# Fewer unread TensorE products in two loops of a graph kernel

## The reference

```
# relational attention, for each of five edge types r
e      = leaky(Qn[tgt] @ a_q + Kn[src] @ a_k)
e_exp  = exp(e - segment_max(e, tgt)[tgt])
attn   = e_exp / (segment_sum(e_exp, tgt)[tgt] + 1e-10)
h     += segment_sum(mask * Vn[src] * attn, tgt)
...
# typed attention, eight heads of 16 features
ex     = exp(scores - segment_max(scores, dst)[dst])
den    = segment_sum(ex, dst)
agg    = segment_sum(V[src] * ex / (den[dst] + 1e-10), dst)
```

## Time and profile before

| what | value |
|---|---|
| median of 3 runs | 4971.89 us (4968.58 to 4981.04) |
| the profiled execution's own time | 4978.06 us |
| its span, first to last instruction | 4976.0 us |
| mean granted TensorE clock over the span | 0.734 |
| TensorE busy / weight loads | 3122.3 us (63%) / 2741.5 us (55%) |
| VectorE, GpSimd, ScalarE busy | 2700.0, 2927.5, 721.8 us |
| last relational loop, first sum to last | 2908.46 to 3188.60 us |
| second typed loop, first sum to last | 3918.02 to 4243.84 us |

### The profile page before, as it was taken

The page is one execution under the profiler, slowest core; times in us unless marked ns, Lnnn a source line. Parts: engine busy times, 40 slices in busy tenths (PEclk is TensorE's granted clock), DMA queues, the critical chain, the costliest instruction groups (busy, mean ns, idle before and its releaser), DMA issues.

```text
span 4976.0 us, 85301 instructions
## 1 busy us (share of the span) xinstructions
PE 3122.3 (63%) x20716; PEld 2741.5 (55%) x20717; DVE 2700.0 (54%) x8043; ACT 721.8 (15%) x1742; POOL 2927.5 (59%) x2911
## 2 busy tenths in 40 slices
PE   0000098886777767776664557767777788667776
PEld 0000088885666656666454346545555688566665
DVE  5100088885444444444667955546666566655553
ACT  1000022222111111111110034420000000411111
POOL 3767677774777747777057877037777000067772
PEclk9999999997555555555765589875555699888886
DMA  6333255554222232223276279476656444033332
GB/s 218 75 89 77 74 154 148 156 153 88 79 76 76 74 61 76 76 75 76 71 208 175 85 199 227 118 206 173 171 171 170 96 126 126 5 91 92 91 92 45
DMA packets 643811, 577.27 MB, mean 116 GB/s; under 512 B 235163, under 2 KB 535800, under 8 KB 643576
## 3 DMA queue, kind: packets, MB, share of 16 engines
q0 software_dynamic: 99328, 211.51, 18.2%
q1 hardware_dynamic: 389624, 235.01, 16.3%
q10 hardware_dynamic: 154752, 129.55, 9.4%
HBM read 424.35 MB, written 151.40 MB: 116 GB/s over the span
## 4 chain that ended last, share of the span: by engine, by line
POOL 50%; issue 20%; PE 14%; DMA 8%; DVE 5%; ACT 1%; SPq 1%; DVEq 0%; POOLq 0%; ACTq 0%
POOL ring L811 29%; POOL HA L829 8%; POOL arena L838 8%; POOL slot_records L797 5%; PE ps L2282 3%; PE ps L2131 2%; DMA ring<-table_gine,idx 2%; DMA arena<-in_edge_attr 2%; DMA table_rel<-arena 1%; PE ps L2283 1%; PE ps L2149 1%; PE ps L2245 1%; DMA slot_records<-arena,slotr 1%; PE ps L1950 1%; DVE HA L854 1%
## 5 line engine op out<-in xcount | busy, mean ns | idle before, releaser
L811 POOL DMA_INDIRECT ring<-table_gine,idx x1248 | 1249.6, 1001 | 498.3 <-issue 370.2
L811 POOL DMA_INDIRECT ring<-table_msg,idx x416 | 398.3, 958 | 630.3 <-DMA table_msg<-arena 503.7
L854 DVE TENSOR_TENSOR mraw<-ps,ring 128x512 f32<-128x512 f32 x416 | 287.7, 691 | 779.4 <-DMA ring<-table_gine,idx 344.1
L838 POOL DMA_INDIRECT arena<-table_keys_values,idx x416 | 435.2, 1046 | 335.8 <-DVEq L186 207.3
L1993 PE MATMUL ps<-oh,msg 128*128 128x128 f32 x1664 | 423.4, 435 | 317.6 <-DVE HA L854 222.8
L829 POOL DMA_INDIRECT HA<-table_rel,idx x416 | 447.1, 1075 | 292.0 <-DMA table_rel<-arena 165.4
L1993 PEld LDWEIGHTS ps<-oh,msg 128*128 128x128 f32 x1664 | 364.5, 323 | 376.2 <-DVE HA L854 345.2
L854 DVE TENSOR_TENSOR HA<-HA,ps 128x128 f32 (+1 forms) x1664 | 476.3, 286 | 165.7 <-DVE HA L854 146.3
L1960 PE MATMUL ps<-wt,ear 65*128 65x128 f32 x2496 | 518.4, 378 | 16.0 <-DMA ear<-edge_attr_T 15.8
L797 POOL DMA_INDIRECT slot_records<-arena,slotr x400 | 392.8, 982 | 213.7 <-issue 123.2
L1960 PEld LDWEIGHTS ps<-wt,ear 65*128 65x128 f32 x2496 | 491.5, 292 | 16.9 <-issue 16.3
(11 more groups left out here) (379 smaller groups left out, 5911.3 us busy)
## 6 DMA issues: line engine op xcount, KB each, us to landing
ear<-edge_attr_T SPq DMA_DIRECT2D x312, 128.0 KB
ear<-slot_rows ACTq DMA_DIRECT2D x312, 128.0 KB
oh<-slot_rows ACTq DMA_DIRECT2D x104, 256.0 KB
slot_values<-HA SPq DMA_DIRECT2D x104, 256.0 KB
ring<-slot_values ACTq DMA_DIRECT2D x104, 256.0 KB
slot_values<-arena SPq DMA_DIRECT2D x104, 256.0 KB
ring<-slot_values SPq DMA_DIRECT2D x104, 256.0 KB, 3.0
slot_records<-msg SPq DMA_DIRECT2D x32, 650.0 KB, 11.6
```

The costliest lines, as they stand in the source:

```text
L811: pool.indirect_dma_start(out=ring[:, k % 4, j, 0:width], out_offset=None, in_=table[:, :], in_offset=bass.IndirectOffsetOnAxis(ap=idx[:, ...
L838: pool.indirect_dma_start(out=kvring[:, k % 4, j, :], out_offset=None, in_=tab2[:, :], in_offset=bass.IndirectOffsetOnAxis(ap=idx5[:, k * ...
L854: return V.tensor_tensor(o, x, y, op)
```

## The change

In the last relational loop `keep_busy` issues three instead of six products of 368 columns at the end of a batch's sums, and in the second typed loop four instead of nine of 176 columns. The products ahead of the loops stay. No value that is read changes.

```diff
@@ -2149,7 +2149,7 @@
                     ins = M.matmul(psf[:, bass.ds(blocks[j] * D, D)], oh[:, t.s4, j, :],
                                    ring[:, t.s4, j, 0:D], start=False, stop=False)
                 ins.then_inc(qa["sums"], 1)
-                keep_busy(6, 368)
+                keep_busy(3, 368)
             keep_busy(14, 368)
             run(pe, [(8, att_sums), (3, att_lookups)])
             for z in range(7):
@@ -2283,7 +2283,7 @@
                     ins = M.matmul(psf[:, bass.ds(blocks[j] * NHEAD + NPAD, NHEAD)], oh[:, t.s4, j, :], msg[:, t.s4, j, D:W2N],
                                    start=False, stop=False)
                 ins.then_inc(qt["sums"], 1)
-                keep_busy(9, 176)
+                keep_busy(4, 176)
             keep_busy(28, 176)
             run(pe, [(6, tr_into), (3, tr_lookups)])
             for z in range(7):
```

## The result

The changed kernel takes 5059.68 us (median of 4 runs, 5052.48 to 5061.43); the kernel before 4970.24 us in the same comparison. The ratio is 1.0167, with a 95% interval of 1.0136 to 1.0197: 1.7% slower. Forecast were 5062 us and 1.8%.

The account below looks back on a forecast made before the run. TensorE was taken to bound typed batches at 1.2 GHz, its instruction stream at 2.4 GHz. Typed loop and closing products +100 us, relational loop -10 us, on the median 4971.89: 5062 us, range 5035 to 5085.

Parts of the forecast that it names:

- The typed loop at the low clock: Second typed loop at 1.2 GHz throughout: 4.11 us a batch instead of 4.84, 427.0 us in all, +98.7 us.
- The clock does not rise: Second typed loop: with four unread products a batch, the clock stays at 0.50 in the whole loop.
- Nothing gained at the high clock: Typed loop at 2.4 GHz: removing five products gains 0 us, within bounds of 0 and 39 us.
- Rival 3: TensorE is the limit at 2.4 GHz, so each removed product shortens its batch: 86 us less, 4886 us; chance 0.03.
- Closing products: Seven products after the typed loop take 3.16 us at the low clock instead of 1.68: +1.5 us.
- Relational loop: Last relational loop: -10 us, bounds 0 and -14, or +26 us if the clock is lost.
- The mechanism: Relational loop: once in four batches the wait for lookups goes, 7 us; the last batches without lookups give 2.3 us.
- The idle time before the sums at the loop's end: Relational loop, each fourth batch: TensorE's idle time before the sums falls from 1.01 to about 0.7 us.
- The comparison by which the relational loop was held safe: Relational loop after the edit: 0.9 + 0.46 of 2.6 us, against the earlier typed loop's 0.9 + 0.68 of 3.09; clock holds.
- rival 2: Typed loop: the clock rises and falls by turns, costing about half of the 98 us, total 5012 us; chance 0.05.
- The sum: Whole kernel: 4978.06 + 100 - 10 = 5068 us; on the medians' scale 4971.89 + 90 = 5062 us, 1.8% slower.

Follow-up runs that it names:

- nine narrow products: Against the kernel before: typed batches have nine unread products of 78 columns instead of 176, relational loop unchanged; 5078.15 us.
- the dense-start kernel: Against the kernel before: eighteen unread products in each of the first ten typed batches, then four, hardware loop starting later; 5067.48 us.
- the dense start: Against the kernel before: three unread products in the relational loop; twenty in each of the first two typed batches, then nine; 4953.7 us, ratio 0.9959.

## Why the prediction was right, point by point

The typed loop at the low clock. Forecast 4.11 us a batch and 427.0 us; measured 4.11 and 426.6. The step took 0.147 us for an unread product between the rows' 0.141 and 0.153; the line through the kernels with none, four, seven, eight and nine gives 0.146.

The clock does not rise. This was the judgement on which all hung. The stretches of the earlier trace rows that were called on for it are weak evidence, as TensorE is idle for about 30% of them and the typed loop has no gap; the better ground was that the rise took five batches with nine. It held, and the loops with seven, with eight and with nine narrow products show that it was not luck: 472.40, 487.66 and 426.80 us of gapless work at 0.50 brought no rise. The rule of the Trainium skill that was weighed against it ("TensorE: Matmul & The Clock Gate", "What's actually happening"), read as if a loop without idle gaps would go to 2.4 GHz, fails in this case: 426.64 of 426.64 us busy at 0.50. Whether a typed loop rose went with the number of its unread 176-column products (nine, twelve and the dense starts did, up to eight did not); why, these runs do not show.

Nothing gained at the high clock. Forecast 0 within 0 to 39 us; in the changed kernel it had no part, as the typed loop has no stretch at 1.00. The four batches of the dense-start kernel at 1.00 with four products take 3.17 us, no less than before. Rival 3 is out.

Closing products. Forecast +1.5 us, measured +1.5 for them and -0.4 for the whole part behind the loop; a term too small to matter.

Relational loop. Forecast -10 us; -5.8 in the pair of profiles. The profile of before has the shortest loop of the eight profiled kernels with six products (280.1 to 291.6 us, mean 286.9); the four with three have 272.2 to 275.1, mean 274.0. That is -13 us in the mean, and the times of the relational edit alone give -15 (-8 to -26), a little more than forecast. By stretches, the first 66 batches go from 176.5 to 181.6 us down to 170.5 to 173.8, the last 19 from 45.0 to 40.9, and the 18 between, with the waits for gathered values, differ too much among themselves to tell.

The mechanism was mostly the one forecast: after the gathers the loop's end batch fell from 3.22 to 2.85 us, and the last batches from 1.82 to 1.36 us. The other three turns, forecast to stay as they were, fell a little too, from 2.41, 2.50 and 2.24 to 2.30, 2.45 and 2.22 us. How it would show in the rows was forecast wrongly. The idle time before the sums at the loop's end was to fall from 1.01 to 0.7 us, and it is 1.07:

```profile
3152.70 1.15 PE L2149 MATMUL ps<-ring,oh 128*128 128x128 f32 x8 [0.50 <-issue]
...
3155.55 1.15 PE L2149 MATMUL ps<-ring,oh 128*128 128x128 f32 x8 [1.07 <-issue]
```

The wait went: the stream's read of block numbers for the lookups follows the one for the sums after 1.2 us here, as in batches that wait for nothing, and after 1.7 us at the place of the earlier trace rows (reads at 3150.2 and 3151.9 us). The batch is 2.85 us where the earlier trace rows belong to one of 3.22. But 0.46 us of products went too, and idle time is what stands in their place: 1.01 + 0.46 - 0.37 = 1.10. A forecast of idle time must take in the work that leaves.

The comparison by which the relational loop was held safe (its share of wide products after the edit equals that of the typed loop before) came true at three. With one product the clock did not hold (0.76), at little cost.

The rise and fall by turns (rival 2) did not come in the typed loop; it came in the relational one with a single product, where it costs little.

The sum. On the scale of the medians the forecast was +90 us and the measured difference 89.4. Part of this closeness is luck. In the pair of profiles the two edited loops and what follows them give +92.1 us (98.3 - 5.8 - 0.4) against 100 - 10 forecast, and the untouched parts are 8.7 us shorter on top, for which the forecast had no term.

## What to carry to other kernels

Unread products that keep TensorE's clock high acted in this loop as a step, not as a slope: with one fewer than needed all the rest were paid and nothing was had for them (eight: 5139 us, none: 5014 us, nine: 4984 us in the same comparison). So look in the profile for how long the stretch at 0.50 lasts at a loop's start; a long or changing one (20.9 us, 54.8 us) was the sign here that the loop sits at the step. Two dense batches at its start were cheaper than three more products in every batch (ratios 0.9959 and 0.9998, intervals apart). Whether the products cost anything at the high clock is to be measured and not read from TensorE's idle time.

## What the runs showed that had not been expected

Idle time of TensorE before an instruction "issued" late did not mean that added work was free. From four to nine products a batch at 1.00 the length stays (3.17 and 3.09 us); from nine to twelve it grows by the whole duration of the added ones (0.22 us), while idle time for issue stays:

```profile
PE ps L2282 <- issue: 33.4, 69, 0.8
```

This is the line of the table of waits for the typed loop with twelve (3940 to 4250 us: sum, times, longest); TensorE waited for issue 33.0 us in 70 places with nine. One reading is that the stream of instructions is held back once it is far enough ahead of TensorE's work. The Trainium skill gives TensorE a queue of 64 ("TensorE: Matmul & The Clock Gate", the table at its head). A typed batch hands over 32 + 18 + 8 = 58 products and weight loads with nine unread products and 64 with twelve, 48 with four; that fits, but no run here varied the number of instructions at equal work and at 1.00, so the cause is argued and not shown. That handing over the added products takes the time by itself is not excluded either.

The weight loads of the fixed tile cost next to nothing at 0.50: nine products of 78 columns took as long as four of 176 (0.55 and 0.54 us).

The time at which the clock rises with nine products varies between executions whose typed loop is the same: 20.9 us before, 45.1 us with one product in the relational loop, 54.8 us with three. By itself that spreads the kernel's time by up to 12 us. The times fit: with the dense start twelve runs span 16 us (4947.14 to 4963.32), and the kernel before spans 43 us in 17 runs of the same comparison (4957.31 to 5000.45). Why the rise comes when it does is not shown.
